# Weighted values ahead of the side work in the pairs that run alone

## The chip, the cores and the metric

One core of one Trainium2 chip runs the whole program. The time is the device time of one execution in microseconds (us). Three runs of the kernel before gave 3104.85, 3105.05 and 3107.97 us; their median is 3105.05 us.

## The reference

Two layers over x, 8 x 512 tokens of width 256. Each layer adds two branches to x: an attention and a mixture of experts or block of its own, both fed with the normalized x.

```
xn = layernorm(x)
x  = x + attn_L0(xn) + experts_L0(xn)      # 16 heads of 16; key and query of 80; softmax; 8 experts, 4 chosen
xn = layernorm(x)
x  = x + attn_L1(xn) + block_L1(xn)        # sparsemax attention; grouped-key attention (4 key heads, softmax)
                                           # with residual, then 8 experts, 2 chosen
# attention, per batch and head, causal:
scores = q @ k.T * scale ; p = softmax or sparsemax(scores) ; out = p @ v
```

## The kernel before

The three attentions run one after the other over the 8 batches each: `mla` (layer 0), `gqa` (the grouped-key attention of layer 1's block) and `spm` (sparsemax). The unit of work is a **pair** of heads, numbered G = 0 to 191: mla is 0 to 63, gqa 64 to 127, spm 128 to 191. n = G // 8 is the batch step and p = G % 8 the pair in it. Each pair does the following, and the scores of a pair are made twice, in two orientations:

- GpSimd (POOL) stacks query and key of the pair (`stack(G)`), two pairs ahead. TensorE (PE) transposes them (`turn_qk`, tiles Tq and Tk, line 452), ScalarE (ACT) evicts them to qsT and ksT (L1453, L1458, L1459). In gqa two pairs share their keys, so that Tk is made for every second pair only.
- **Query units**: six score units with queries on the partitions (`scores("q", ...)`, masks L524 and matmuls L542), one pair ahead. VectorE (DVE) takes row maxima (L1840; L1838 for sparsemax) and makes the shift of the softmax (`shift`), which it writes into the stacked queries. PE transposes these once more (`shifted`, tile Ta), ACT evicts them to qaT (L1476).
- **Key units**: six units with keys on the partitions (`scores("k", ...)`, L524 and L545), evicted by ACT as exponentials (L1472) into `pt`.
- **Weighted values**: `outputs(G)`, 16 matmuls of pt by V (L621), into tile O; ACT evicts O (`take_o`, L1480); PE transposes it (`outputs_by_rows`, tile N, L452 with oT); DVE sums it up and divides (`heads_out`, L1921 to L1927; L1912 to L1916 for sparsemax). The DVE instruction at L1922 (L1916) releases the bank of N.

**Two kinds of pairs.** In pairs 21 to 49 and 138 to 176 (`plan`) the experts' matmuls run between the pieces of the attention (`pair_with_experts`). All others are **alone** (`pair_alone`): 0 to 20, 50 to 137, 177 to 191. Beside its own pair, a pair alone does **side work** by p: in gqa steps with neighbours on both sides, p = 1 turns the next batch's rows (`turn_rows`) and the former batch's context (`turn_context`); p = 2 makes the former batch's output projection (`attention_out`, L652); p = 2 to 5 project the next batch (L576; then rotated by DVE); p = 5 turns the hidden rows, p = 6 makes logits (L670) and p = 7 ranks (L678). DVE has its side work between `shift(G + 1)` and `heads_out(G - 1)`, and at p = 0 the row statistics of the next batch ahead of its maxima. In pairs 0 to 19 the side work is routing, with scatters on POOL.

**Banks and order.** Every engine runs its instructions in the order in which they are written. Four of the eight PSUM banks are the ring X in a pair alone (all transposes, projections, O and N), four the ring S (the score units). A ring gives its banks in turn; a name waits until the name four places ahead of it in the same ring has been read. So k unit 0 waits for the maximum of q unit 2, k units 1 to 3 for those of q units 3 to 5, k units 4 and 5 for the exponentials of k units 0 and 1; q units 4 and 5 wait for the maxima of q units 0 and 1. `outputs(G - 1)` waits for the last exponential of pair G - 1.

In `scores`, `masks_last` puts the masks behind the matmuls where the ring S has as many banks as there are units; that is so in pairs with experts (three banks, three units) and in the fallback program `general` (six and six).

Of the kernel before, what the change touches and what calls it, by code (L numbers as in the profile page):

```python
# [149 lines left out]
def build(nc, dram, outs, ctx):  # L150
# [164 lines left out]
    def pipeline(kinds, its, mems, em=None, boot=None, general=False):  # L315
# [10 lines left out]
        def is_at(n, kind):  # L326
            return 0 <= n < nb and kinds[n] == kind
# [8 lines left out]
        plan = {}  # L336
# [30 lines left out]
        S = Ring(first_banks[1], {"act": s_act, "dve": s_dve}, last)  # L367
# [63 lines left out]
        with block as block:  # L431

            @block.tensor
            def _(pe):
# [78 lines left out]
                def scores(which, G, units):  # L513

                    mem = mems[kinds[G // NP]]
                    bare = which == "k" and G in plan
                    masks_last = which == "q" and len(S.banks) == len(units)
                    side = 0 if which == "q" else 1

                    def mask(u, start):  # L520

                        unit = (Q_UNITS if which == "q" else K_UNITS)[u]
                        diag = min(first + (P * blk if which == "q" else 0) for _, blk, first, _ in unit)
                        return pe.matmul(S.bank((which, G, u))[:, diag:diag + P * len(unit)], ident_bf[:, :],  # L524
                                         masks_bf[:, side, 0:len(unit), :].rearrange("p n k -> p (n k)"),
                                         start=start, stop=not start, skip_group_check=True)

                    for u in units:
                        name = (which, G, u)
                        S.add(name, "dve" if which == "q" else "act")  # L530
                        if S.former[name]:
                            pe.wait_ge(*S.former[name])
                        bank = S.bank(name)
                        unit = (Q_UNITS if which == "q" else K_UNITS)[u]
                        if not bare and not masks_last:
                            mask(u, True)
                        for n, (j, blk, first, width) in enumerate(unit):
                            begin = n == 0 and (bare or masks_last)
                            end = n == len(unit) - 1 and not masks_last
                            ks = mem["ksT"][key_at[G] % 2][j]  # L540
                            if which == "q":
                                mm = pe.matmul(bank[:, first:first + width], mem["qsT"][:, P * blk:P * (blk + 1)],  # L542
                                               ks[:, 0:width], start=begin, stop=end, skip_group_check=True)
                            else:
                                mm = pe.matmul(bank[:, first:first + width], ks[:, P * blk:P * (blk + 1)],  # L545
                                               mem["qaT"][:, T - width:T], start=begin, stop=end, skip_group_check=True)
                        if not masks_last:
                            mm.then_inc(s_full, 1)
                    if masks_last:
                        for u in units:  # L550
                            mask(u, False).then_inc(s_full, 1)
# [32 lines left out]
                def turn_q(name, G):  # L584
                    qs = mems[kinds[G // NP]]["qst"][G % 2]
                    turn(name, "act", [qs[:, t, :, :].rearrange("p j n -> p (j n)") for t in range(NT)])
# [10 lines left out]
                def shifted(G):  # L597

                    pe.wait_ge(shift_ready, G + 1)
                    turn_q(f"Ta{G}", G)  # L600
# [174 lines left out]
                def pair_alone(G):  # L775
                    n, p = divmod(G, NP)
                    if G + 1 < steps:
                        turn_qk(G + 1)
                    shifted(G)
                    if n + 1 < nb and p == 1:  # L780
                        turn_rows(n + 1)
                    if routes(G, 0):
# [18 lines left out]
                    if G + 1 < steps:  # L801
                        keys_in(G + 1)
                        scores("q", G + 1, range(NU))
                    if G and G - 1 not in plan:
                        outputs(G - 1)
                    pe.wait_ge(x_act, X.count[f"Ta{G}"])
                    scores("k", G, range(NU))
                    if G:
# [542 lines left out]
            def _(act):  # L1351
# [122 lines left out]
                def take_qa(G):  # L1474
                    act.wait_ge(x_full, X.full(f"Ta{G}"))
                    act.activation(mems[kinds[G // NP]]["qaT"][:, :], X.bank(f"Ta{G}")[:, :], ACT.Copy).then_inc(x_act, 1)  # L1476

                def take_o(G):
                    act.wait_ge(x_full, X.full(f"O{G}"))
                    act.activation(mems[kinds[G // NP]]["oT"][:, :], X.bank(f"O{G}")[:, :], ACT.Copy).then_inc(x_act, 1)  # L1480
# [86 lines left out]
                def pair_alone(G):  # L1567
                    n, p = divmod(G, NP)
                    if is_at(n - 1, "gqa") and p == 7:
                        exponents(n - 1)  # L1570
                    if G + 1 < steps:
                        take_qk(G + 1)
                    take_qa(G)
                    if n + 1 < nb and p == 1:
                        take_rows(n + 1)
                    if routes(G, 0):
# [15 lines left out]
                            take_turned("Th", n - 1)  # L1592
                    if is_at(n - 1, "spm") and p == 1:
                        take_turned("Tc", n - 1)
                    if G and G - 1 not in plan:
                        take_o(G - 1)
                    probabilities(G, range(NU))
                    if is_at(n, "gqa") and 1 <= p <= 3:
                        split_high(n, p - 1)
# [912 lines left out]
```

## Time and profile before

| what | value |
|---|---|
| median of 3 runs | 3105.05 us |
| the profiled execution's own time | 3129.51 us |
| its span | 3127.6 us |
| PE busy | 90% |
| DVE, ACT, POOL busy | 68%, 52%, 48% |
| granted TensorE clock, mean | 0.956 |

The page divides the span by engine; a busy PE can be one that runs at half clock. The windows give busy times by stage, the timeline gives instructions in order with the idle time ahead of them and what ended it, in brackets.

### The profile page before, as it was taken

What the parts mean: (1) busy time and instruction counts of PE and PEld (TensorE: products, weight loads), DVE (VectorE), ACT (ScalarE), POOL (GpSimd) and SP (SyncE); (2) the same over time, 40 slices, a digit from 0 to 9 for tenths busy, and PEclk for the clock granted to TensorE, in tenths of its full rate; (3) what the DMA queues carried; (4) which work ended last, traced back from release to release, by engine and by line L of the source; (5) the groups of instructions that cost most, each with busy time, mean ns of one, the idle gap of its engine ahead of it and who ended that gap; (6) DMA issues with size and microseconds to landing.
All of it is one profiled execution on the core that took longest, in us unless ns stands there. A gap on an engine that the chain in (4) does not pass through costs nothing. (4 is left out here: it accounts for less than half of the span.)

```text
span 3127.6 us, 61182 instructions
## 1 busy us (share of the span) xinstructions
PE 2809.4 (90%) x20990; PEld 2275.6 (73%) x20990; DVE 2133.4 (68%) x6013; ACT 1615.2 (52%) x3388; POOL 1506.6 (48%) x2213
## 2 busy tenths in 40 slices
PE   5877799999999999978998898998799999999996
PEld 3555478888899889846666666666588888888864
DVE  6878678788788788767777877766644444454565
ACT  3544344444454445545655555655455555555553
POOL 4768743443343354385556666322233333332487
PEclk8878799999999999989999999999899999999998
DMA  3555578788888888422333344210466666665355
GB/s 83 197 208 202 196 262 311 278 286 316 284 290 307 294 286 308 178 40 55 97 99 104 105 107 109 93 69 22 164 213 210 228 213 212 204 241 203 124 97 126
DMA packets 212008, 580.13 MB, mean 185 GB/s; under 512 B 24617, under 2 KB 146417, under 8 KB 167409
## 3 DMA queue, kind: packets, MB, share of 16 engines
q1 hardware_dynamic: 172528, 523.82, 47.7%
q0 software_dynamic: 36864, 51.14, 8.1%
q8 instruction: 172, 2.82, 0.4%
q10 hardware_dynamic: 2304, 1.21, 0.1%
q14 instruction: 140, 1.14, 0.1%
HBM read 450.14 MB, written 125.96 MB: 184 GB/s over the span
## 5 line engine op out<-in xcount | busy, mean ns | idle before, releaser
L1139 POOL TENSOR_TENSOR al<-t,ah 128x512 fp32r<-128x512 f32 x220 | 283.4, 1288 | 875.1 <-ACT ah L1375 875.1
L481 PE MATMUL bank<-xh,gu 128*128 128x256 f32 x3520 | 672.3, 291 | 33.6 <-DVE gc L1654 25.8
L481 PEld LDWEIGHTS bank<-xh,gu 128*128 128x128 f32 x3520 | 512.6, 190 | 57.7 <-issue 55.0
L524 PE MATMUL bank<-masks_bf,ident_bf 128*128 128x128 bf16 x1896 | 432.9, 252 | 133.9 <-DVE st L1840 41.0
L1840 DVE TENSOR_REDUCE st<-bank 128x1 f32<-128x512 f32 (+3 forms) x1024 | 422.1, 481 | 166.1 <-PE bank L542 158.6
L1472 ACT ACTIVATE pt<-bank 128x512 f32<-128x512 f32 (+1 forms) x1152 | 512.0, 540 | 30.2 <-PE bank L545 21.9
L524 PEld LDWEIGHTS bank<-masks_bf,ident_bf 128*128 128x128 bf16 x1896 | 170.3, 99 | 353.6 <-DVE st L1840 95.3
L1480 ACT ACTIVATE oT<-bank 128x512 f32<-128x512 f32 x192 | 114.6, 597 | 602.5 <-PE bank L621 576.5
L542 PE MATMUL bank<-ksT,qsT 128*128 128x512 f32 (+3 forms) x1536 | 410.3, 369 | 5.7 <-DVE top L1838 3.1
L545 PE MATMUL bank<-qaT,ksT 128*128 128x512 f32 (+3 forms) x1536 | 399.6, 372 | 0.0
L481 PE MATMUL bank<-xl,gu 128*128 128x256 f32 x1760 | 351.5, 281 | 0.0
L1375 ACT ACTIVATE ah<-t 128x512 fp32r<-128x512 f32 x220 | 138.9, 631 | 399.6 <-DVE t L1680 358.7
L542 PEld LDWEIGHTS bank<-ksT,qsT 128*128 128x128 f32 x1536 | 278.7, 202 | 28.2 <-DVE top L1838 17.8
L452 PE MATMUL bank<-ident,qst 128*128 128x128 f32 x1536 | 236.9, 282 | 54.2 <-POOL kst L1193 37.8
L545 PEld LDWEIGHTS bank<-qaT,ksT 128*128 128x128 f32 x1536 | 268.2, 201 | 6.0
L481 PEld LDWEIGHTS bank<-xl,gu 128*128 128x128 f32 x1760 | 270.5, 189 | 0.0
L1838 DVE MAX8 top<-bank 128x8 f32<-128x512 f32 (+3 forms) x512 | 213.9, 484 | 82.9 <-PE bank L542 60.6
L621 PE MATMUL bank<-pt,V 128*17 128x512 f32 (+3 forms) x3072 | 263.0, 463 | 0.9 <-ACT pt L1472 0.7
L499 PE MATMUL bank<-dn,ah 128*128 128x256 f32 x1760 | 257.7, 289 | 1.6 <-ACT yb L1388 0.8
L452 PEld LDWEIGHTS bank<-ident,qst 128*128 128x128 f32 x1536 | 184.9, 145 | 83.4 <-issue 47.4
L499 PEld LDWEIGHTS bank<-dn,ah 128*128 128x128 f32 x1760 | 223.1, 189 | 9.7 <-issue 8.4
L1246 POOL DMA_INDIRECT acc<-ys_scratch,slots x128 | 203.4, 1589 | 44.4 <-issue 44.0
(250 smaller groups left out, 5216.2 us busy)
## 6 DMA issues: line engine op xcount, KB each, us to landing
gu<-wu_scratch SPq DMA_DIRECT2D x110, 1032.0 KB, 5.2
gu<-wu_scratch SPq DMA_DIRECT2D x110, 1024.0 KB, 7.4
dn<-wd_scratch SPq DMA_DIRECT2D x110, 1024.0 KB, 6.7
xs<-xs_scratch SPq DMA_DIRECT2D x110, 264.0 KB, 4.3
ys_scratch<-yb SPq DMA_DIRECT2D x110, 256.0 KB, 7.0
raw<-in_gu SPq DMA_DIRECT2D x16, 1024.0 KB
wu_scratch<-hi SPq DMA_DIRECT2D x16, 1024.0 KB
wu_scratch<-lo SPq DMA_DIRECT2D x16, 1024.0 KB
```

The lines of the kernel that those rows point to most:

```text
L452: mm = pe.transpose(bank[:, P * n:P * (n + 1)], b, ident[:, :])
L481: mm = pe.matmul(bank[:, TS * h:TS * (h + 1)], gu[:, col:col + P], x[s % 2][:, TS * k:TS * (k + 1)], start=(n == 0), stop=(n == len(terms) ...
L499: mm = pe.matmul(down_bank[:, D * half:D * (half + 1)], a[s % 2][:, j // 2, tok:tok + P], dn[:, part + D * j:part + D * (j + 1)], start=(n ...
L524: return pe.matmul(S.bank((which, G, u))[:, diag:diag + P * len(unit)], ident_bf[:, :], masks_bf[:, side, 0:len(unit), :].rearrange("p n k ...
L542: mm = pe.matmul(bank[:, first:first + width], mem["qsT"][:, P * blk:P * (blk + 1)], ks[:, 0:width], start=begin, stop=end, skip_group_che ...
L545: mm = pe.matmul(bank[:, first:first + width], ks[:, P * blk:P * (blk + 1)], mem["qaT"][:, T - width:T], start=begin, stop=end, skip_group ...
L621: mm = pe.matmul(bank[q0:q0 + HD + 1, P * kb:T], V[n % 2][:, kb, vh, :], pt[:, j, PT_AT[kb]:PT_AT[kb] + T - P * kb], start=(kb < 2), stop= ...
L1139: pool.tensor_tensor(em["al"][s % 2][:, m, :], em["t"][g % 2][:, :], em["ah"][s % 2][:, m, :].bitcast(F32), ALU.subtract).then_inc(al_read ...
L1246: pool.indirect_dma_start(acc[:, NT * b + t, :], None, ys_dram, at, compute_op=ALU.add).then_inc(gathered[i], 16)
L1472: act.activation(to, frm, ACT.Relu if kind == "spm" else ACT.Exp).then_inc(s_act, 1)
L1838: ins = dve.max(top[:, 0, r, :], bank[:, first:first + width])
L1840: ins = dve.reduce_max(st[:, 0, r:r + 1], bank[:, first:first + width], AX.X)
```

## The change

In pairs alone, `outputs(G - 1)` on PE and `take_o(G - 1)` on ACT move. Before, they stand behind the query units of pair G + 1 and ahead of the key units of pair G. After, they stand ahead of the side work and of the query units: in mla and gqa right behind `shifted(G)` and `take_qa(G)`, in spm ahead of them, between Tq/Tk of pair G + 1 and Ta of pair G. With this, O takes another place in the order of the ring X. The condition of `masks_last` is written in another way. The first pair behind a stage with experts has no such work to move, and DVE, POOL and the DMA queues keep their order.

```diff
-                    masks_last = which == "q" and len(S.banks) == len(units)
+                    masks_last = which == "q" and (G - 1 in plan or general)
...
                     if G + 1 < steps:
                         turn_qk(G + 1)
-                    shifted(G)
+                    if is_at(n, "spm"):
+                        if G and G - 1 not in plan:
+                            outputs(G - 1)
+                        shifted(G)
+                    else:
+                        shifted(G)
+                        if G and G - 1 not in plan:
+                            outputs(G - 1)
...
                     if G + 1 < steps:
                         keys_in(G + 1)
                         scores("q", G + 1, range(NU))
-                    if G and G - 1 not in plan:
-                        outputs(G - 1)
                     pe.wait_ge(x_act, X.count[f"Ta{G}"])
                     scores("k", G, range(NU))
...
                     if G + 1 < steps:
                         take_qk(G + 1)
-                    take_qa(G)
+                    if is_at(n, "spm"):
+                        if G and G - 1 not in plan:
+                            take_o(G - 1)
+                        take_qa(G)
+                    else:
+                        take_qa(G)
+                        if G and G - 1 not in plan:
+                            take_o(G - 1)
...
-                    if G and G - 1 not in plan:
-                        take_o(G - 1)
                     probabilities(G, range(NU))
```

## Rows read from the trace of the kernel before

**Rows 1.** Windows by stage: length; PE, PEld, DVE, ACT, POOL busy; PEclk, DMA, GB/s.

```profile
0.00:425.00 425.00, 315.41 (x1788) 218.31 (x1789) 300.56 (x878) 185.68 (x374) 283.06 (x325) 0.81 0.53 183
425.00:1322.00 897.00, 857.03 (x6997) 797.30 (x6995) 725.43 (x1644) 433.71 (x870) 375.18 (x485) 1.00 0.80 287
1322.00:2236.00 914.00, 803.30 (x5808) 559.58 (x5807) 666.56 (x2114) 521.37 (x1176) 480.62 (x736) 0.95 0.31 81
```

**Rows 2.** Waits between 1322 and 2236: us in total, times, longest.

```profile
DVE st L1840 <- PE bank L542: 104.8, 48, 6.8
PEld bank L524 <- DVE st L1840: 69.9, 180, 3.7
PEld bank L524 <- ACT ksT L1459: 24.0, 30, 1.2
```

**Rows 3.** Windows of gqa pairs 104, 106 and 107 (p = 0, 2, 3).

```profile
1865.70:1878.10 12.40, 9.41 (x59) 5.98 (x58) 9.82 (x39) 4.73 (x11) 5.88 (x10) 0.72 0.14 46
...
1888.70:1901.00 12.30, 11.89 (x78) 8.52 (x77) 8.10 (x23) 5.93 (x16) 7.27 (x10) 1.00 0.20 34
1901.00:1910.40 9.40, 8.91 (x65) 6.01 (x66) 8.98 (x25) 8.03 (x24) 1.90 (x4) 1.00 0.00 0
```

**Rows 4.** Timeline of PE, pair 106: start, us, instruction [idle before].

```profile
1894.39 0.48 PE L542 MATMUL bank<-ksT,qsT 128*128 128x512 f32 x1
...
1896.65 1.27 PE L621 MATMUL bank<-pt,V 128*17 128x512 f32 x16
1897.89 0.47 PE L545 MATMUL bank<-qaT,ksT 128*128 128x512 f32 x1
...
1900.18 0.60 PE L452 MATMUL bank<-ident,oT 128*128 128x128 f32 x4
...
1901.98 0.66 PE L452 MATMUL bank<-ident,kst 128*128 128x128 f32 x4 [0.34 <-DVE xb_gqa L1953]
```

**Rows 5.** Timeline of DVE, pair 106: maxima, and the release of N.

```profile
1894.91 3.27 DVE L1840 TENSOR_REDUCE st<-bank 128x1 f32<-128x512 f32 x8 [3.13 <-PE bank L542]
...
1902.63 0.26 DVE L1922 TENSOR_TENSOR both<-both,bank 128x102 f32<-128x102 f32 x1
```

**Rows 6.** Timeline of PE, pairs 104 and 105 (p = 0, 1).

```profile
1871.26 0.40 PE L524 MATMUL bank<-masks_bf,ident_bf 128*128 128x256 bf16 x1 [2.71 <-DVE st L1840]
1872.46 2.34 PE L621 MATMUL bank<-pt,V 128*17 128x512 f32 x16
...
1877.64 0.60 PE L452 MATMUL bank<-ident,oT 128*128 128x128 f32 x4
...
1880.98 1.09 PE L452 MATMUL bank<-ident,hrow 128*128 128x128 f32 x8 [1.44 <-DVE hrow L1763]
```

**Rows 7.** Timeline of DVE, pair 104.

```profile
1870.52 3.27 DVE L1840 TENSOR_REDUCE st<-bank 128x1 f32<-128x512 f32 x8
...
1874.86 1.38 DVE L1751 TENSOR_SCALAR xb_gqa<-acc,stats 128x256 f32<-128x256 f32 x4
1878.27 0.30 DVE L1921 COPY both<-bank 128x136 f32<-128x136 f32 x1 [2.04 <-PE bank L452]
```

**Rows 8.** Timeline of PE, pair 62, with no side work.

```profile
1452.40 0.23 PE L524 MATMUL bank<-masks_bf,ident_bf 128*128 128x128 bf16 x1 [0.92 <-ACT ksT L1459]
```

**Rows 9.** Timeline of PE, pair 54.

```profile
1373.32 0.39 PE L524 MATMUL bank<-masks_bf,ident_bf 128*128 128x256 bf16 x1 [3.39 <-DVE st L1840]
```

**Rows 10.** Timeline of DVE in the first stage, pairs 4 and 15.

```profile
111.22 3.28 DVE L1840 TENSOR_REDUCE st<-bank 128x1 f32<-128x512 f32 x8 [2.92 <-PE bank L542]
...
321.33 0.30 DVE L1921 COPY both<-bank 128x136 f32<-128x136 f32 x1 [4.05 <-PE bank L452]
```

**Rows 11.** Timeline of POOL, pair 181.

```profile
3003.33 0.29 POOL L1174 CAST qst<-qk 128x128 fp32r<-128x128 f32 x1 [1.76 <-PE bank L452]
```

**Rows 12.** The chain that ended last, in order of time: start, us, engine, line.

```profile
3009.33 1.54 POOL acc L1269
...
3111.97 1.54 POOL acc L1269
```

## The prediction

> **What bounds the kernel now.** First the windows by stage: the stages with experts between (425 to 1322 shown) have PE busy 857 of 897 us at full clock; nothing in them is edited [rows 1]. The edit works in pairs alone: 121 pairs, of which 87 lie in the 914 us from 1322 to 2236, with PE busy 88% and DVE 73% [rows 1]. Then the waits of that stretch: DVE waits 104.8 us for query units, PE 69.9 us for row maxima and 24.0 us for the eviction of the keys [rows 2]. So neither engine is the bound alone: it is a loop through both. The windows of single pairs show how close they lie: in pair 107 PE is busy 8.91 and DVE 8.98 of 9.40 us [rows 3]. What limits the time is therefore how long it takes from the first query unit of one pair to the first of the next ("q0 to q0"), and I read that off the timelines.
>
> **Three paths in a pair alone.** (1) PE alone: q0 at 1894.39, weighted values (O) at 1896.65, key units at 1897.89, N at 1900.18 [rows 4]: q0 to N is 5.8 us, of which O takes 1.24 from its start to the next. (2) The key units' wait: DVE begins its maxima 0.52 us behind q0 and needs 3.27 us for six units [rows 4, 5]. Now O and what follows cover that. With O gone from there, key unit 1 comes up before the maximum of query unit 3 is there, and unit 3 waits for the last maximum: N can't come before q0 + 0.55 + 3.3 + 0.1 (the semaphore) + 1.0 (three key units, half of the 2.05 us that the six take in a pair without waits) = q0 + 5.0. So of the 1.24 us that O leaves behind, I take 0.6 to come back as N earlier and 0.6 to be lost (bounds: 0, where N stays, and 1.24, were DVE not there). (3) DVE: from q0 through maxima, shift, side work and heads_out to the release of N's bank: 1902.63 + 0.26 - 1894.39 = 8.5 us [rows 4, 5].
>
> **What the moved O does at its new place.** It comes up at the end of Ta, when the last exponential is there (in a regular pair at about Tq + 0.8, and Ta ends at Tq + 1.0 to 1.5). It then stands ahead of q0 with its 1.24 us. Three cases:
>
> - *No side work.* PE idles 0.92 us for ksT there [rows 8]; O fills it. q0 moves by 0.3, N comes 0.3 earlier. These pairs gain 0.3 us each.
> - *Side work, PE dense.* q0 moves by 1.24, N by 0.65: q0 to q0 grows by 0.65.
> - *Side work, release of N late.* Replaying the order of the ring X, O now stands four places behind N of the pair before in nearly all gqa pairs (p = 3, 5, 7), or the side work does (p = 6), and Ta waits for the projection's banks (p = 3; today's 0.34 us wait for L1953 is that one [rows 4]). Then path (3) is the loop, and O lies on it behind the release and ahead of q0. The whole 1.2 us are added, and N's earlier coming is worth nothing.
>
> **The sum, gqa.** For a batch step with all side work, q0 to q0: p = 1 to 2 dense +0.65; 2 to 3 path (3) +1.2 (8.5 + 0.1 + O 1.24 + projection 1.3 = 11.1 against 10.0 now); 3 to 4 dense +0.6; 4 to 5 path (3) +1.2; 5 to 6 path (3), through the logits, +1.2; 6 to 7 path (3), where PE has some idle time, +0.45; 7 to 0: DVE's own chain, 0. Together +5.3. Then p = 0 to 1 gives back: there the maxima start late, PE idles 2.71 us, falls to half clock (O takes 2.34 us; granted clock of the pair 0.72), and N comes at 1877.64 [rows 3, 6]. DVE then idles 2.04 us for N, and the next rows (L1763) and PE's 1.44 us wait hang on that [rows 6, 7]. With O ahead of the gap, N could come at 1870.52 + 3.27 + 1.1 = 1874.9, ahead of DVE's end with L1751 at 1876.24, so that those 2.0 us go [rows 7]. Six such steps (pairs 72 to 119): 6 x 5.3 = 31.8; the return is 2.0 four times, 1.35 once, 0 in the first: -9.4. Sum +22.4.
>
> **The other stretches.** Pairs 56 to 71, few sides: +1.2 (seven pairs with a projection at some +0.5, five without at -0.3 to -0.5, and one late release). 120 to 127: +1.0 and -2.0: -1. Pairs 51 to 55: two have PE waiting over 3 us for maxima [rows 9] and O at half clock; -4. 128 to 137: sides +0.65 each, three pairs with a late DVE at about -2: -2.3. The last stage: from pair 181 the chain is POOL's without a break [rows 12], started by the Ta that POOL waits 1.76 us for [rows 11]. In spm, O stands ahead of Ta, so this anchor comes 1.25 us later, against 3 x 0.35 us from pairs 178 to 180: +0.2; what pairs 182 to 190 gain is hidden by POOL. The first stage (pairs 1 to 20) is a mesh of routing on DVE, POOL and ACT: q0 comes up to 1.2 us later where DVE waits for it (2.92 us in pair 4), N up to 3 us earlier where O runs at half clock behind late maxima (DVE idles 4.05 us in pair 15) [rows 10]. By some ten waits of each kind I take -3, with +8 and -12 as ends. Half-clock O's are 19 in all, at 150.4 to 2233.8, and 18 of them stand behind or beside a late maximum.
>
> ACT: O's eviction (0.6 us) goes ahead of the side's evictions; ACT is busy 521 of 914 us [rows 1] and I cost it 0, or 0.3 us a pair if a projection waits for it (+10 on 35 pairs, upper end). DVE and POOL keep their order; POOL's stack waits for Ta, which moves in spm alone. `masks_last`: three units on three banks are exactly the calls with G - 1 in the plan, six on six the fallback; nothing changes. No DMA is moved.
>
> Total: 22.4 + 1.2 - 1 - 4 - 2.3 + 0.2 - 3 = +13.5 us. The profiled execution's own time, 3129.5, becomes 3143; it is 24.5 us above the median of the runs, and I put the same difference on the median: 3105.05 + 13.5 = 3118.5.
>
> **The clock.** The pair with the 2.71 us gap has a granted clock of 0.72, that is, it changes between the levels of 2.4 and 1.2 GHz, and pairs without a gap stand at 1.00 [rows 3, 6]. The Trainium skill, "TensorE: Matmul & The Clock Gate", What's actually happening, says that the clock is set by how busy the engine has been recently. By that, O ahead of the gap makes PE busier before it, and it may stay at full clock; the sum above has the gap as long as now, so the fall stays. By the page it would be some 6 us lower, to about 3112.
>
> **Rivals.**
>
> 1. *No change (18%).* The releases of N are not late after all: an earlier N pulls heads_out forward by as much as O pushes. Then the four late steps cost 0.65, 0.65, 0.65 and 0 instead of 1.2, 1.2, 1.2 and 0.45: 2.1 us less on each of six batch steps, -12.6; total +1, 3106. For it: in many pairs N comes at q0 + 5.8 to 6.2 today, so more than 0.6 could come back. Against: pair 107 has DVE at 96% [rows 3], and path (3) there doesn't go through N at all.
> 2. *Faster (24%).* Half clock is the dear part: each of the 19 slow O's has 1.1 us of its own and some 0.9 us of slow key units, and a moved O spares both wherever PE waits for maxima [rows 6, 9]. If all 19 give 2.5 us, that is -47 where I counted about -31; with rival 1's term, 13.5 - 16 - 12.6 = -15: 3090. It decides if the first stage follows N rather than q0. Against it: DVE waits longer in sum for query units than for N in the stretch that I can read.
> 3. *Slower still (10%).* As forecast, but the first stage follows q0 (+8 in place of -3) and ACT's earlier eviction holds projections up (+10): +34, 3139.
> 4. *That the change doesn't do what it says* has no room: the order is written out.
>
> **How the numbers follow.** Forecast 48% (own range 3110 to 3128), rival 3 10%, rival 1 18%, rival 2 24%. Range for 8 in 10: 3088 to 3138. 0.2% (6.2 us) is what a measurement of this kernel can tell from no change. Slower by over 0.2% (above 3111.3): the forecast's and rival 3's 58%; what the forecast's lower edge loses, rival 1's upper edge adds. Within: 0.18. Faster: 0.24.
>
> **What would show it.** In gqa at p = 3, 5 and 7, idle time ahead of L621 with L1922 as its releaser, and pair 106's q0 to pair 107's q0 at 11.1 us against 10.0; key masks (L524 ahead of L545) waiting for L1840; the pair without side work 0.3 us shorter; p = 0 ending with O at 1.24 us and DVE's 2.04 us wait gone; POOL's chain at the end as long as before. The forecast is wrong if gqa pairs at p = 2 to 6 don't get longer, and wrong in size if the first stage moves by over 10 us.

## The result, and the profile after

The changed kernel takes 3143.34 us (median of 4 runs, 3138.16 to 3145.27) against 3104.95 us before; the ratio is 1.0122, 95% interval 1.0107 to 1.0138. It is slower, as forecast, but by 38 us and not by 13.5; 3143.3 lies above the range's end of 3138.

In what follows a **slot** G is the code of `pair_alone(G)`; its first query unit, q0, is that of pair G + 1, as in the prediction. The lines of the changed kernel stand 5 to 10 further down: L1922 is now L1932, L1459 is L1464, L1840 is L1850. The experiments' kernels stand 8 lines further on PE (L621 is L629) and 18 to 23 on DVE (L1922 is L1940 or L1942, L1840 is L1858, L1860 or L1863).

The stretch from 1322 to 2236 us answers to [rows 1] and [rows 2]: first its window, then its waits (us in total, times, longest). PE isn't less busy than before (816 against 803 us, with fewer matmuls in it), and both waits of the loop through DVE have grown, from 104.8 to 165.6 and from 69.9 to 102.6 us; that for ksT, 24.0 us before, is 1.4.

```profile
1322.00:2236.00 914.00, 816.11 (x5687) 555.29 (x5686) 648.27 (x2061) 532.72 (x1153) 470.49 (x719) 0.96 0.30 78
```

```profile
DVE st L1850 <- PE bank L542: 165.6, 64, 8.9
PEld bank L524 <- DVE st L1850: 102.6, 280, 3.3
...
PEld bank L524 <- ACT ksT L1464: 1.4, 6, 0.3
```

Now the pair that the prediction walked through, pair 106, on PE. The view is the timeline: start, us, instruction, idle before and its releaser.

```profile
1901.19 0.47 PE L542 MATMUL bank<-ksT,qsT 128*128 128x512 f32 x1
...
1903.56 0.48 PE L545 MATMUL bank<-qaT,ksT 128*128 128x512 f32 x1
...
1906.06 0.60 PE L452 MATMUL bank<-ident,oT 128*128 128x128 f32 x4
...
1907.72 0.66 PE L452 MATMUL bank<-ident,kst 128*128 128x128 f32 x4 [0.63 <-DVE xb_gqa L1963]
1908.87 0.63 PE L452 MATMUL bank<-ident,qst 128*128 128x128 f32 x4 [0.50 <-DVE xb_gqa L1963]
1909.84 1.27 PE L621 MATMUL bank<-pt,V 128*17 128x512 f32 x16 [0.34 <-DVE both L1932]
1911.04 1.56 PE L576 MATMUL bank<-w_gqa,xT 128*128 128x384 f32 x4
...
1912.46 0.48 PE L542 MATMUL bank<-ksT,qsT 128*128 128x512 f32 x1
```

The reader is to see three things. N comes at q0 + 4.87 us (1906.06 - 1901.19; it was 5.8 in [rows 4], and 5.0 was expected). O now waits 0.34 us for DVE's release of N's bank. And q0 to q0 is 11.27 us; 11.1 was expected and 10.0 was the measure before. DVE's release is the second line here:

```profile
1909.10 0.29 DVE L1931 COPY both<-bank 128x136 f32<-128x136 f32 x1
1909.43 0.26 DVE L1932 TENSOR_TENSOR both<-both,bank 128x102 f32<-128x102 f32 x1
```

At p = 0 (slot 104, PE and then DVE) the wait for late maxima stays (2.49 us, 2.71 in [rows 6]), but no O lies behind it at half clock. The O of the next pair takes 1.27 us, DVE waits 0.18 us for N and not 2.04 [rows 7], and the wait for L1773 (`hrow`) is 0.24 us in place of 1.44 [rows 6].

```profile
1879.16 0.28 PE L524 MATMUL bank<-masks_bf,ident_bf 128*128 128x256 bf16 x1 [2.49 <-DVE st L1850]
1883.68 0.60 PE L452 MATMUL bank<-ident,oT 128*128 128x128 f32 x4
1885.52 1.27 PE L621 MATMUL bank<-pt,V 128*17 128x512 f32 x16
1887.03 1.09 PE L452 MATMUL bank<-ident,hrow 128*128 128x128 f32 x8 [0.24 <-DVE hrow L1773]
```

```profile
1884.32 0.30 DVE L1931 COPY both<-bank 128x136 f32<-128x136 f32 x1 [0.18 <-PE bank L452]
```

The windows of slots 104 to 107, from q0 to q0, have columns as in [rows 1]; ahead of them stands slot 104 in the trace of before, cut in the same way. (The 0.72 of [rows 3] is of another stretch, from the start of the slot's code.) The granted clock of slot 104 was 0.78 and is 0.87; the section on the prediction says why this can't be put down to the change. PE has 1.70 us of idle time in slot 106 and 0.24 in slot 107.

```profile
1867.10:1882.82 15.72, 11.57 (x78) 8.13 (x78) 11.16 (x42) 7.18 (x14) 9.60 (x16) 0.78 0.23 55
```

```profile
1875.19:1888.83 13.64, 10.77 (x81) 7.95 (x77) 10.98 (x41) 7.40 (x14) 8.24 (x12) 0.87 0.10 14
1888.83:1901.16 12.33, 12.09 (x78) 8.57 (x76) 6.16 (x16) 6.94 (x16) 10.56 (x17) 1.00 0.26 52
1901.16:1912.43 11.27, 9.57 (x65) 5.99 (x64) 9.72 (x25) 6.57 (x12) 3.29 (x6) 1.00 0.21 37
1912.43:1921.32 8.89, 8.65 (x62) 5.54 (x61) 7.38 (x22) 7.38 (x21) 2.62 (x2) 1.00 0.00 0
```

### The profile page after: what moved, and what is told of

It reads as the page before. It is cut to its first block and busy times, and to the rows that moved or that the text cites. A ratio compares the mean times of both kernels' runs of the same rounds, so it can differ in the third digit from the quotient of the medians.

```text
span 3143.6 us, 61182 instructions
## 1 busy us (share of the span) xinstructions
PE 2840.9 (90%) x20990; PEld 2273.4 (72%) x20990; DVE 2134.3 (68%) x6013; ACT 1643.1 (52%) x3388; POOL 1511.9 (48%) x2213
## 3 DMA queue, kind: packets, MB, share of 16 engines
q14 instruction: 139, 1.14, 0.1%
## 5 line engine op out<-in xcount | busy, mean ns | idle before, releaser
L1477 ACT ACTIVATE pt<-bank 128x512 f32<-128x512 f32 (+1 forms) x1152 | 526.8, 527 | 341.9 <-PE bank L545 333.3
L1850 DVE TENSOR_REDUCE st<-bank 128x1 f32<-128x512 f32 (+3 forms) x1024 | 421.9, 482 | 237.6 <-PE bank L542 232.1
L524 PE MATMUL bank<-masks_bf,ident_bf 128*128 128x128 bf16 x1896 | 430.3, 250 | 60.4 <-DVE st L1850 26.3
L545 PE MATMUL bank<-qaT,ksT 128*128 128x512 f32 (+3 forms) x1536 | 432.5, 376 | 0.0
L542 PE MATMUL bank<-ksT,qsT 128*128 128x512 f32 (+3 forms) x1536 | 403.0, 364 | 5.7 <-DVE top L1848 3.1
L452 PE MATMUL bank<-ident,qst 128*128 128x128 f32 x1536 | 244.6, 288 | 110.3 <-POOL kst L1198 71.8
L542 PEld LDWEIGHTS bank<-ksT,qsT 128*128 128x128 f32 x1536 | 272.6, 198 | 31.0 <-DVE top L1848 17.8
L621 PE MATMUL bank<-pt,V 128*17 128x512 f32 (+3 forms) x3072 | 260.1, 458 | 17.6 <-DVE both L1932 11.8
```

Source lines behind the costliest of these rows:

```text
L452: mm = pe.transpose(bank[:, P * n:P * (n + 1)], b, ident[:, :])
L621: mm = pe.matmul(bank[q0:q0 + HD + 1, P * kb:T], V[n % 2][:, kb, vh, :], pt[:, j, PT_AT[kb]:PT_AT[kb] + T - P * kb], start=(kb < 2), stop= ...
L1477: act.activation(to, frm, ACT.Relu if kind == "spm" else ACT.Exp).then_inc(s_act, 1)
L1850: ins = dve.reduce_max(st[:, 0, r:r + 1], bank[:, first:first + width], AX.X)
```

## The experiments

All kernels are the changed one, with the place of O asked of one function. Its eviction on ACT moves with it in the changed kernel's own rule; in the rules "sides" and "amid" below it stays at its old place.

```diff
+        def o_at(G):
+            n, p = divmod(G, NP)
+            if not G or G - 1 in plan:
+                return None
+            moved = "ahead" if is_at(n, "spm") else "behind"   # of Ta, as in the change
+            return RULE                                        # "old": between query and key units
```

**Which part costs what (e1 to e4).** The rules:

```diff
+            return "old"                                       # e1_old
+            return moved if G < 21 else "old"                  # e2_first
+            return moved if 72 <= G < 128 else "old"           # e3_gqa
+            return moved if G >= 128 else "old"                # e4_spm
```

> Every weighted value stands where it stood before: the instructions are those of the kernel before. Both theories expect a ratio of 1.000. What is open is its trace. Theory A (the profiled execution of before was typical but for a constant): a span of about 3127 and the same time of each stage as in the trace of before. Theory B (the 24.5 us that the profiled execution had above the median of its runs lie in single pairs, at half clock or late maxima, and a usual execution doesn't have them, so that the change can't give them back): a span near 3104, with most of the 24 us less lying in pairs 0 to 20 and 50 to 57, where the trace of after is 15 and 6 us ahead of that of before.

> Moved in pairs 1 to 20 alone. Theory A: 3 us faster by the forecast, up to 15 us by the two traces laid side by side. Theory B: nothing is given back in a usual execution, 0 to +8 us.

> Moved in the grouped-key pairs 72 to 127 alone. Theory A: +21.4 us (the forecast's term for these pairs). Theory B: the forecast took 9.4 us for given back at p = 0; if a usual execution has those waits too, +21; the two traces show +28 here (from 18.0 us ahead to 10.0 behind), and as the whole is +38, this part is +28 to +32.

> Moved in the sparsemax pairs 128 to 137 and 178 to 191 alone, where it stands ahead of Ta. Theory A: -2.1 us (-2.3 and +0.2). Theory B: the two traces show +5.7 in pairs 128 to 137 and -4.2 behind pair 176, of which the second is of the profiled execution alone: +4 to +6.

Before took 3103.33 us here. e1_old: 0.9997 (0.9988 to 1.0006), span 3101.3. e2_first: 1.0013 (1.0003 to 1.0022), +4 us. e3_gqa: 1.0099 (1.0083 to 1.0114), +31 us. e4_spm: 0.9998 (0.9989 to 1.0007). So most of the loss is the grouped-key part, and the first stage adds to it where the forecast had -3. The sparsemax part is within the noise (-3 to +2 us): it fits theory A's -2.1 and not theory B's +4 to +6, which had been read off two traces of different length.

The trace of e1_old is that of the same instructions as before, and it is 26.3 us shorter than the one that the prediction was read from. 18.2 of these lie in front of slot 21, 1.3 in slots 21 to 50, 1.3 in 51 to 55, 3.7 in 56 to 71, 0.5 in 72 to 127, 1.4 behind. One example is slot 7, from q0 to q0: first in the trace of before, then in that of e1_old.

```profile
160.70:189.06 28.36, 19.58 (x93) 14.32 (x94) 19.63 (x61) 8.88 (x16) 20.93 (x28) 0.70 0.77 279
```

```profile
160.60:179.60 19.00, 15.56 (x93) 11.61 (x92) 17.57 (x52) 9.50 (x17) 15.14 (x20) 0.78 0.97 350
```

The waits of before between 80 and 440 us (total, times, longest) name a releaser that the e1_old trace doesn't have in that stretch at all:

```profile
ACT oT L1480 <- remote: 19.5, 4, 5.2
DVE both L1921 <- remote: 6.9, 1, 6.9
POOL qst L1174 <- remote: 4.0, 2, 2.1
```

Theory B holds on this: the 24.5 us were no constant of profiling but time of the first stage, above all. The next four runs bear on where they come from.

**How the places differ (e5 to e8).** In e8 DVE's order is changed too.

```diff
+            return moved if 64 <= G < 128 and p == 0 else "old"    # e5_p0
+            return "sides" if 72 <= G < 128 else "old"             # e6_sides: behind the side work
+            return "amid" if 72 <= G < 128 else "old"              # e7_amid
+                    if o_at(G) == "amid":
+                        scores("q", G + 1, range(NU // 2))
+                        outputs(G - 1)
+                        scores("q", G + 1, range(NU // 2, NU))
# e8_rotate: the rule of e3, and on DVE, for 72 <= G < 120 and p = 2 to 5 (twice at p = 5):
-                            rotate(n + 1, p - 2)
                     if G:
                         heads_out(G - 1)
+                            rotate(n + 1, p - 2)
```

> Moved at p = 0 of the grouped-key batch steps alone (pairs 64, 72, ..., 120: eight of them), where the query units wait for late maxima. Theory A (the return at p = 0 is real in a usual execution, and the push comes from the other pairs): p = 0 to 1 shorter by 1.4 us and a little more, as its next O stays behind its query units (2.0), p = 7 to 0 longer by 0.2 as in the trace of after: -1.8 us on each of seven steps, -10 to -13 us, 3092. Theory B (nothing is given back in a usual execution): 0 to +2 us.

> In pairs 72 to 127 O stands behind the side work and ahead of the query units, so that the ring X gives its banks in the order of before. Theory A (O is costly because it stands ahead of the first query unit, on the path release of N, side work, O, q0): no change against the moved version, +26 to +30 us. Theory C (the order of the ring X is the cause: O now waits for the release of N four places ahead): with the old order the p = 3 and p = 5 steps lose their +1.2, -2 to -3 us on each of six steps, +12 to +18 us. Where the projection is ahead of O at PE and its banks are free sooner, theory A would see up to 0.5 us less a pair at p = 4 and 5.

> In pairs 72 to 127 O stands behind the third of the six query units. Theory A (a loop through DVE from the first query unit): the maxima start when they did before, the key units start when they did before: 0 us, at most 0.3 us a pair where the fourth maximum now waits for its unit (+5). Theory D (what costs is that O is gone from between query and key units, so that nothing covers the key units' wait for the maxima, whatever stands ahead of q0): 0.65 us in each pair remain, +25 us or more.

> As the change in pairs 72 to 127, and DVE's rotation of the projected rows (five instructions, 1.5 us a pair at p = 2 to 5) stands behind heads_out in place of ahead of it, so that the bank of N is released 1.5 us earlier. Theory A (path 3, the release of N, bounds p = 2, 4 and 5): these steps fall from +1.2 and more to the +0.65 of the dense ones, -0.5 to -0.8 each, some -2 us on each of six steps: +18 us in place of the +30 of the same move without the rotation. Theory E (the release of N is not on the path, PE's own dense work is): unchanged, +30 us.

These four ran on another chip, on which the kernel before took 3132.34 us (21 runs, 3124.26 to 3139.74). The first chip had 3097.6 to 3106.85 in 27 runs. The profiled execution of before, 3129.51 us, fits the second kind, while the three runs shown beside it fit the first. In the trace of e5_p0, q0 of slot 21 comes at 436.1 us, against 430.5 in the trace of before and 412.3 in that of e1_old, and the grouped-key steps agree with those of the first chip (10.04 and 10.05 us at p = 2). Waits with the releaser "remote" between 80 and 440 us stand in the traces of before, e5 to e8, e17 and e18, whose q0 of slot 21 comes at 430 to 439 us, and in none of the thirteen others. So the trace of before is very likely one of the second kind; its chip isn't known.

e5_p0: 0.9981 (0.9968 to 0.9993), -6 us. e6_sides: 1.0126 (1.0107 to 1.0145), +39 us. e7_amid: 1.0076 (1.0059 to 1.0092), +24 us. e8_rotate: 1.0023 (1.0008 to 1.0037), +7 us. What they say is read step by step. Each row is the mean length of q0 to q0 in slots 80 to 119 (five batch steps), worked out from the starts of L542 (L550) in the timelines; all rows but the first are differences from it. Each is read from one execution. How far that goes is shown by the rows of before and e2_first, where O stands at its old place in these slots: p = 1 to 6 repeat within 0.15 us, p = 0 and p = 7 don't.

| slot p to p + 1 | 0 | 1 | 2 | 3 | 4 | 5 | 6 | 7 | sum |
|---|---|---|---|---|---|---|---|---|---|
| e1_old, us | 15.35 | 11.57 | 10.05 | 8.24 | 11.00 | 8.60 | 9.56 | 7.36 | 81.7 |
| before | -0.20 | 0.15 | 0.00 | 0.00 | 0.01 | 0.12 | -0.13 | 0.25 | 0.2 |
| e2_first | -0.84 | 0.00 | 0.00 | 0.00 | 0.01 | 0.00 | -0.11 | 0.51 | -0.4 |
| forecast | -2.0 | 0.65 | 1.2 | 0.6 | 1.2 | 1.2 | 0.45 | 0 | 3.3 |
| changed kernel | -1.39 | 0.77 | 1.23 | 0.65 | 1.14 | 1.47 | 0.38 | 0.22 | 4.5 |
| e5_p0 | -2.08 | 0.08 | 0.00 | 0.00 | 0.00 | 0.13 | -0.14 | 0.91 | -1.1 |
| e6_sides | -0.10 | 0.68 | 1.33 | 0.56 | 1.31 | 0.90 | 0.38 | 0.25 | 5.3 |
| e7_amid | -0.46 | 0.10 | 0.66 | -0.09 | 1.77 | -0.02 | 0.65 | 1.66 | 4.3 |
| e8_rotate | -1.26 | 0.77 | -0.17 | 0.86 | -0.68 | 0.70 | 0.30 | 0.27 | 0.8 |
| e10_rotate_old | 0.04 | 0.00 | -0.77 | 0.57 | -0.28 | -0.07 | 1.39 | 0.00 | 0.9 |
| e11_both | -2.12 | 0.00 | -0.77 | 0.57 | -0.29 | -0.07 | 1.07 | 0.85 | -0.8 |
| e12_hole | -1.10 | -0.52 | -0.65 | 2.12 | 1.12 | 0.70 | 0.28 | 0.22 | 2.2 |
| e13_p0_72 | -2.50 | 0.00 | 0.00 | 0.00 | 0.01 | 0.00 | -0.01 | 1.35 | -1.1 |

- *e5_p0.* The gain is there but smaller than the 10 to 13 us expected: what p = 0 gives (2.1 us a step) is in part taken back at p = 7 (0.9 us, where 0.2 was expected): the moved O stands ahead of the q0 that ends this step.
- *e6_sides.* The order of the ring X is that of before, and p = 2 and 4 lose 1.33 and 1.31 us: theory C falls, and so does part of my own words for it. That O's bank waits for the release costs nothing; that O stands on PE between that release and q0 costs 1.2. At p = 0 this version also loses the return; the likely reason, not tried by itself, is that O now stands behind `turn_rows` of slot 105, which waits for DVE.
- *e7_amid.* p = 1, 3 and 5 are back at 0, though O is gone from between query and key units: among the query units it still fills the time in which DVE takes its maxima. Theory D, by which 0.65 us a pair would remain, falls. But theory A's "0" fails as well. The two groups of maxima of pair 106 are apart, because unit 4 comes 1.2 us later:

```profile
1910.29 1.68 DVE L1863 TENSOR_REDUCE st<-bank 128x1 f32<-128x512 f32 x4 [3.34 <-PE bank L550]
1912.55 1.68 DVE L1863 TENSOR_REDUCE st<-bank 128x1 f32<-128x512 f32 x4 [0.58 <-issue]
```

  The last maximum ends at q0 + 4.46 us (1909.77 is q0) in place of 3.80, and these 0.66 us are what p = 2 grows by. PE waits there for the residual (L1976, 1.16 and 0.34 us) and not for N's release, so at p = 2 path (3) already binds at the residual's release of its banks. Why p = 4 and p = 7 grow by 1.7 I haven't followed.
- *e8_rotate.* With DVE's rotation out of the way, the releases come 1.5 us earlier (at p = 5, where two rotations or ten instructions move, about 3 us). That takes 1.40, 1.82 and 0.77 us from p = 2, 4 and 5 of the moved version, nothing from p = 1, and adds 0.21 at p = 3. Theory A; theory E falls. The residual's release and N's move together here, so that the two aren't told apart. In its slot 106 PE's idle time is 0.57 us, where the changed kernel had 1.70:

```profile
1900.94:1910.81 9.87, 9.30 (x66) 5.99 (x65) 8.90 (x25) 6.32 (x12) 2.88 (x6) 1.00 0.19 37
```

**The changed kernel again, and the rotation alone (e9 to e12).** Before took 3103.64 us here.

```diff
# e9_after: as changed.  e10_rotate_old: rule "old" and e8's rotation.
# e11_both: e5's rule and e8's rotation.  e12_hole: e8, and on PE, for 72 <= G < 120 and p = 2 to 4:
-                        project(n + 1, p - 2)
                         scores("q", G + 1, range(NU))
+                        project(n + 1, p - 2)
                     scores("k", G, range(NU))
```

> The changed kernel once more. Theory F (two chips differ in pairs 0 to 20, where the trace of before came from the one that needs 3124 to 3140 us for the kernel before, and the change gives part of that back only there): ratio 1.012 on a chip where before takes 3097 to 3107 us, and 1.005 to 1.009 on one where it takes 3124 to 3140, as the changed kernel would then need about 3145 to 3160. Theory G (the chip moves both kernels alike): 1.012 on either, 3142 or 3170.

> Every weighted value at its old place; only DVE's rotation stands behind heads_out in pairs 72 to 119. Theory A (the release of N bounds p = 2 and p = 4 in the kernel before too, where PE idles 0.34 and 1.03 us for it): -0.3 and -1.0 us on these steps, -1.3 on each of six, some -8 us, 0.997. Theory E (what the rotation gave in the kernel with the move was that kernel's own late release): 0 us.

> The move at p = 0 alone (pairs 64, 72, ..., 120) and the rotation behind heads_out (72 to 119). If the two are independent: -1.1 us a step from the first (measured) and -1.3 from the second, -14 us, 0.995. If the second one's gain is lost again in the wait at p = 0: -6 us as the first alone.

> The kernel with the move and the rotation behind heads_out in pairs 72 to 127 (1.0023 when timed), and in addition PE's projection at p = 2 to 4 stands between query and key units, where O stood. Theory A (in the dense pairs the move costs 0.65 us because nothing covers the key units' wait for the maxima): the projection covers it, -0.6 us at each of p = 2, 3, 4, 18 pairs: -10 us against that kernel, 0.999. Theory D (what a piece ahead of q0 costs is its own time, the wait is worth nothing): the projection's 1.4 us and not 0.6 come back, -4 us a step, -25, 0.994. Theory H (it is only put off: the rotation now waits for the later projection): 0 or longer, 1.002 to 1.004.

- *e9_after*: 1.0111 (1.0096 to 1.0127), 3138.4 us. The chip was of the first kind, so F and G are not told apart: no run of the changed kernel fell on the second kind.
- *e10_rotate_old*: 1.0017 (1.0007 to 1.0026), +5 us where I expected -8. The gain at p = 2 is there (-0.77, more than twice what I gave it), and that at p = 4 is -0.28 of the -1.0 I gave it. They are lost at p = 3 and p = 6: the rotation now lies ahead of the next pair's maxima, which then start late. At p = 6 PE waits for them ahead of its fifth query unit:

```profile
1913.71 0.28 PE L532 MATMUL bank<-masks_bf,ident_bf 128*128 128x256 bf16 x1 [1.07 <-DVE st L1858]
```

- *e11_both*: 1.0002 (0.9993 to 1.0011). A step of e5 (-1.1) and one of e10 (+0.9) would make -0.2, and -0.8 was measured: part of the rotation's loss at p = 6 is lost in the same wait. The rotation isn't worth having with O at its old place.
- *e12_hole*: 1.0044 (1.0030 to 1.0058), +14 us. At p = 2 the step is 0.48 us shorter than in e8 (theory A said 0.6), but p = 3 and 4 are 1.3 and 1.8 longer. ACT evicts the projection ahead of the exponentials, and so these start only when the later projection is there; key unit 4 waits for the exponential of key unit 0. At p = 3, shown here, 1.6 us of ACT's work on the hidden rows (L1509) stand between the two as well:

```profile
1892.48 0.28 PE L532 MATMUL bank<-masks_bf,ident_bf 128*128 128x256 bf16 x1 [1.41 <-ACT pt L1488]
```

  None of the three theories had this; H had the sign and the size, but another wait.

**The cause of both prices, and the faster versions (e13 to e16).** Before took 3103.46 us.

```diff
+            return moved if 72 <= G < 128 and p == 0 else "old"    # e13_p0_72
+            return moved if 50 < G < 72 else "old"                 # e14_51_71
# e15_short_old (rule "old") and e16_short_moved (rule of e3), for 72 <= G < 128:
-                                ins = dve.reduce_max(st[:, 0, r:r + 1], bank[:, first:first + width], AX.X)
+                                ins = dve.reduce_max(st[:, 0, r:r + 1], bank[:, first:first + width // 2], AX.X)
+                        act.activation(to, frm, ACT.Exp, scale=1e-4)
```

> Moved at p = 0 of the seven batch steps with all side work alone (pairs 72, 80, ..., 120), without pair 64, where the eighth move of the run before it brought +1.3 us. Theory A: -1.2 us a step (p = 0 -2.1, p = 7 +0.9), -2.0 at 72: -9 us, 0.997. Theory B: 0.

> Moved in pairs 51 to 71 alone. By the forecast: -4 for pairs 51 to 55 and +1.2 for 56 to 71, -2.8 us, 0.999. By the traces of the changed kernel laid beside the usual one of before: 0 for pairs 51 to 55 and +5 for 56 to 71, less 2 to 3 us at pair 72, whose wait for the moved rows is then shorter: +3 to +5 us, 1.001 to 1.0016.

> Base for the next run, every weighted value at its old place: in pairs 72 to 127 the row maxima are taken over half the columns (so that DVE needs some 2 us and not 3.27 for a pair), with the exponential's argument scaled by 0.0001 to stay in range; the output of these pairs is another. Both theories: steps bound by PE alone (p = 3) keep their 8.24 us; p = 2 and 4 lose the wait for the release of N, 9.7 and 10.0.

> The same short maxima with the move in pairs 72 to 127, read against the run before it, step by step. Theory A (both costs, the key units' uncovered wait and the late release of N, come from the row maxima): p = 1 and p = 3 grow by 0 to 0.2 us in place of 0.77 and 0.65, p = 2, 4 and 5 by 0 to 0.4 in place of 1.23, 1.14 and 1.47. Theory D (a piece on PE ahead of the query units costs as such): the steps grow as before, +0.65 and +1.2.

- *e13_p0_72*: 0.9978 (0.9969 to 0.9987), -7 us where I expected -9: faster than both kernels. Slots 103 and 104 in its windows, where the e1_old trace had 7.36 and 15.79 us:

```profile
1833.01:1841.21 8.20, 8.06 (x73) 5.33 (x74) 6.95 (x29) 4.62 (x10) 4.39 (x4) 1.00 0.42 96
1841.21:1854.88 13.67, 9.99 (x66) 7.66 (x62) 10.56 (x39) 6.97 (x13) 8.85 (x14) 0.88 0.17 32
```

- *e14_51_71*: 1.0008 (0.9999 to 1.0017), +2.5 us; by the trace -1.2 in 51 to 55 and +4.0 in 56 to 71. The forecast's -2.8 lies outside.
- *e15_short_old and e16_short_moved* took 0.9873 and 0.9913 of before (two runs each). With short maxima the steps are 13.85, 11.29, 9.00, 7.94, 10.01, 8.26, 8.56, 7.01 us, and the move adds -0.89, +0.11, +1.07, +0.01, +1.08, +0.51, +0.95, -0.44. In e15 itself p = 3 is 7.94 us and not the 8.24 that I took for PE's alone, and p = 2 is 9.00 and not 9.7: DVE had a larger part in both than I thought. Slots 106 and 107, e15 first, then e16:

```profile
1848.78:1857.77 8.99, 8.87 (x66) 5.86 (x65) 8.02 (x25) 5.63 (x12) 4.45 (x7) 1.00 0.26 46
1857.77:1865.70 7.93, 7.93 (x61) 5.41 (x62) 5.87 (x23) 7.24 (x22) 3.24 (x3) 1.00 0.00 0
```

```profile
1852.82:1862.89 10.07, 8.85 (x66) 5.96 (x65) 8.53 (x25) 6.27 (x12) 3.68 (x6) 1.00 0.23 41
1862.89:1870.84 7.95, 7.95 (x62) 5.53 (x61) 6.12 (x22) 7.22 (x21) 2.68 (x2) 1.00 0.00 0
```

  p = 1 and 3 answer theory A: 0.11 and 0.01 in place of 0.77 and 0.65. So the price in dense pairs is the key units' wait for maxima. p = 2 and 4 don't: 1.07 and 1.08, not 0.4; p = 6 grows by more than with full maxima (0.38), which I haven't followed. By size alone p = 2 and 4 fit theory D, a price of the piece as such. But by theory D PE would be busy throughout, and in e16's slot 106 it is idle for 1.22 of 10.07 us. It still waits for the same three releases, by DVE's residual (L1973) and by the release of N (L1942):

```profile
1858.16 0.65 PE L460 MATMUL bank<-ident,kst 128*128 128x128 f32 x4 [0.39 <-DVE xb_gqa L1973]
1859.31 0.63 PE L460 MATMUL bank<-ident,qst 128*128 128x128 f32 x4 [0.50 <-DVE xb_gqa L1973]
1860.27 1.27 PE L629 MATMUL bank<-pt,V 128*17 128x512 f32 x16 [0.34 <-DVE both L1942]
```

  The maxima are 1.26 us shorter on this path (2.01 and not 3.27), and the moved step 1.2 us shorter (11.27 to 10.07): the path is path (3), and shortening it shortens the step by as much. The price stays because the step without the move gets 1.05 us shorter too. Not enough was taken off for PE to take over; the expectation's size was wrong, its path wasn't.

**Further places of that kind (e17, e18).**

```diff
+            return moved if 72 <= G < 128 and p == 0 or G == 137 else "old"          # e17_p0_137
+            return moved if 72 <= G < 128 and p == 0 or G in (55, 137) else "old"    # e18_p0_137_55
```

> The faster version (moved at p = 0 of pairs 72 to 120) and pair 137 moved too, behind which the trace of the changed kernel has 4.2 us less, after 2.0 more at 136. Theory A (a move gives time back wherever it stands ahead of a late maximum, by its own): -2 us more, 0.997. If what pair 137 gained hung on the moves of the pairs before it: 0.998 as without it.

> As the run before, with pair 55 moved too, where the trace of the changed kernel has 3.7 us less after some 1.6 more at 54. Theory A: -2 us more than the run before, 0.9965. If the gain at 55 hung on pairs 52 to 54: 0 or up to +1 us.

Before took 3132.68 us here, so the chip was of the second kind. e17: 0.9976 (0.9966 to 0.9985). e18: 0.9965 (0.9952 to 0.9979). Both beat the kernel before; e13, e17 and e18 can't be told from each other. In the trace of e17 slots 135 to 137 are 2.2 us shorter than in that of before (-0.94, +1.55, -2.83), as expected. The -0.94 isn't the move's, as slot 135 is as short (9.65 us) in e2_first and e3_gqa; but the sum of the three, 58.2 us, is 1.5 us below the shortest of all traces with O at its old place there (59.7 to 60.7). In e18 slots 54 to 57 have +0.32, -0.71, +0.55, +0.19 against before, where e17 has -0.01, -1.14, -0.01, +0.68: pair 55 by itself gives nothing, and e18's smaller ratio doesn't come from there.

## Why the prediction was right in sign and wrong in size

By stretch, against the trace of e1_old (differences between starts of q0; the changed kernel's own trace / that of e9_after):

| slots | forecast | measured |
|---|---|---|
| 1 to 20 | -3 | +7.7 / +3.6 |
| 21 to 50 | 0 | +2.4 / +0.6 |
| 51 to 55 | -4 | +0.1 / -1.6 |
| 56 to 71 | +1.2 | +5.0 / +5.9 |
| 72 to 127 | +21.4 | +29.9 / +29.5 |
| 128 to 137 | -2.3 | -4.6 / -4.0 |
| behind | +0.2 | +1.8 / +1.8 |
| sum | +13.5 | +42.3 / +35.8 |

These are single executions. Where no O is moved, traces of the first kind of chip spread over 3.3 us in slots 21 to 50, 2.3 in 51 to 55, 3.2 in 56 to 71 and 5.3 in 72 to 127 (e2_first is the shortest there). The timed runs by part say +4 for the first stage (e2_first), +2.5 for 51 to 71 (e14_51_71), +31 for 72 to 127 (e3_gqa) and 0 for the sparsemax part (e4_spm), together close to the 38.

**Bounds and paths: right.** Both prices of the grouped-key pairs came out: dense pairs 0.65 and 0.77 us (forecast 0.65), pairs on path (3) 1.23 and 1.14 (forecast 1.2), p = 6 0.38 (0.45). e7, e15 and e16 show that the first is the uncovered wait for maxima; e8 and e16 show that the second is DVE's late release of banks, the residual's and then N's. N at q0 + 4.87, q0 to q0 of 11.27, the waits for L1932 ahead of O (16 of them in slots 50 to 137, 11.8 us, 15 of them at p = 3, 5 and 7) and the end of the half-clock O at p = 0 are as the last part of the prediction asked for.

**The failed step: the first stage's "-3", and the constant behind it.** The prediction took N to come earlier "where O runs at half clock behind late maxima" and set this above q0 coming later where DVE waits for it. The runs show the reverse. q0 of slot 21 comes at 409.9 to 413.7 us in the ten traces of the first kind of chip in which O stands at its old place in this stage, and at 415.9 to 420.0 in the three in which it is moved. O's of over 1.6 us are two to four in those ten (six in the trace of before), and twelve or thirteen in those three: in this stage the moved O doesn't get away from the half clock but comes to stand in it. And DVE's waits for query units between 80 and 440 us grow from 34.6 us (e1_old) to 50.0:

```profile
DVE st L1850 <- PE bank L542: 50.0, 16, 5.1
```

How much of the 4 to 8 us comes from either isn't measured.

The same step fails where it goes from the trace to the timed runs: "it is 24.5 us above the median of the runs, and I put the same difference on the median". I took the difference for a constant. It was 18 us of the first stage and some 6 of slots 21 to 71, very likely on a kind of chip that the timed runs were not on, and gains booked against these waits can't be given back where the waits don't occur. That bears on the "-3" and in part on the "-4" of pairs 51 to 55. No kernel with O moved in the first stage ran on the second kind of chip, so what the change does there is open.

These terms are less than half of the miss of 25 us: 7 us of it by the timed run of the first stage, 5 by that of slots 51 to 71. Another 10 (e3_gqa; 8 by the traces) are sizes in slots 72 to 127, where the difference between the kinds of chips has no part (0.5 us between the traces of before and e1_old).

The two traces of before and after side by side say +16 us, close to the 13.5. That this agrees is luck, as they are of two kinds of chip: they have the first stage at -10.5 and slots 72 to 127 at +29.4.

**Mis-sized terms of the sum.** In slots 72 to 119 the pushes are 5.9 us a batch step and not 5.3 (p = 5 has 1.47, not 1.2; p = 7 has 0.22, not 0): +3.8 over six. The returns at p = 0 are -9.8 us in all (forecast -9.4), which is luck: the first batch step, put at 0, gives 2.9, and the other five, put at 9.4, give 7.0. The last batch step, 120 to 127, was forecast at +1.0 - 2.0 and took +4.2: its p = 0 gives nothing back (+0.22), and the pushes are 4 us. Together these are the 8.5 us by which this stretch was undersized. In slots 56 to 71 seven of the pairs with side work cost 0.63 to 0.78 and not "some +0.5", slot 61 costs 1.38, and the pairs without side work gave -0.59, +0.21, -0.36 and +0.22, not -0.3 to -0.5 each. The terms that the prediction names there also add up to more than its +1.2: 3.5 - 2 + 1.2 for the late release is 2.7.

**The rivals.** Rival 1 (the releases are not late) falls with e8: with an earlier release the steps get shorter. Rival 2 (half clock is the dear part) falls: with no half-clock O left in slots 72 to 127 this stretch is 30 us longer, and in the first stage their number grows. Its kernel of truth is e13, which takes only the places where O lay behind late maxima. Rival 3 is nearest in time (3139), and half of it is right: the first stage's +8 is the upper end of what was measured. Its ACT term isn't seen at p = 3: the eviction of O is earlier in e3 too, and its step has just the 0.65 that e16 takes to 0.01 with ACT's order unchanged. At p = 5 it isn't ruled out: e6_sides, with O's eviction at its old place, has 0.90 us there and the changed kernel 1.47, but O's place on PE differs too. `masks_last` costs nothing to be seen (e1_old is at 0.9997). What lies behind slot 137 took +1.8 us and not +0.2.

**The clock.** The granted clock of slot 104, q0 to q0, is 0.78 in the traces of before and e1_old and 0.87 in that of the changed kernel. The Trainium skill, "TensorE: Matmul & The Clock Gate", What's actually happening, says that the clock follows how busy the engine has been recently. These rows don't settle whether O ahead of the gap made the difference: in e2_first, with O at its old place, slot 104 has 0.89 (below), and over slots 72 to 127 the clock is 0.97 in e1_old and 0.96 in the changed kernel. What the move spares is that O itself falls into the slow stretch (2.34 us before, 1.27 after). That the page's rule would save 6 us more was not seen.

```profile
1846.14:1861.29 15.15, 10.81 (x77) 7.46 (x78) 11.21 (x42) 6.96 (x14) 9.42 (x16) 0.89 0.22 47
```

## What to carry to other kernels

A piece of work between two groups of matmuls may be a cover: ask what the second group waits for, and what stands between a late release and the instruction that starts the next round. The same move loses 1.2 us where it lies on the path from the release to the next first unit, 0.65 us where it uncovers a wait, and gives 2.1 to 2.5 us where it leaves a stretch behind a late maximum, of which the step before takes 0.9 to 1.4 back: make it by place, not for all pairs. And when the profiled execution's own time doesn't fit the timed runs, book no gains in the stretches with waits that occur only there. Where several executions of one kernel are traced, compare them first: a step that moves by 0.8 us without any change can't show a gain of 0.5.

## What the hardware showed that was not expected

- Two kinds of chips: for the same kernel before, 3097.6 to 3108.5 us in 69 runs on three of them, and 3124.3 to 3139.7 in 38 runs on two. Each was used for one set of runs, so that the chip and the time of the run aren't told apart. Most of the difference lies in front of slot 21 (against e1_old 18 us of 26 in the trace of before, 20 for e17, 27 for e18), in a stage where only the slow kind has waits that the trace puts down to "remote". What they are is open.
- Grouped-key steps repeat closely on either kind of chip: p = 2 takes 10.03 to 10.07 us in slots 74 to 114, in the kernel before and in e1, e2, e4, e5 and e13.
- Moving DVE's rotation behind the release won 0.8 us at p = 2, where it is five instructions (1.5 us), and cost 1.4 us at p = 6, behind p = 5, where it is ten.
